# Four graph layers on one core: exponent rows through DMA, multi-head aggregation transposed for head pairs, new order of work

## What is computed

```python
h = relu(layernorm(x)); x = x + L0(h)     # one head: softmax(mask(leaky_relu(h W1 (h W2)^T))) (h W3), relu
h = relu(layernorm(x)); x = x + GAT(h)    # 4 heads of 64: e = leaky_relu(e_src_i + e_dst_j), softmax, elu
h = relu(layernorm(x)); x = x + MHA(h)    # 4 heads of 64, biases, output projection Wo, layernorm * gamma + beta
h = relu(layernorm(x)); x = x + GAT(h)    # as layer 1, other weights
```

## Time and profile before

| | before |
|---|---|
| median of 3 runs | 3149.03 us (3148.59 to 3149.07) |
| profiled execution | 3149.14 us, span of the core 3147.3 us |
| TensorE busy | 3024.6 us, 96% |
| VectorE busy | 2164.3 us, 69% |
| ScalarE busy | 1628.3 us, 52% |
| GpSimd busy | 765.3 us, 24% |
| mean granted TensorE clock | 0.988 |

### The profile page before, as it was taken

One profiled execution on the slowest core, in us unless ns is written; L12 is line 12 of the kernel. 1 busy time (PEld: TensorE's weight loads), 2 busy tenths in 40 slices (PEclk: granted clock), 3 DMA queues, 4 the chain that ended last, 5 costly groups with the idle time before them and its releaser, 6 DMA issues.

```text
span 3147.3 us, 83725 instructions
## 1 busy us (share of the span) xinstructions
PE 3024.6 (96%) x35494; PEld 2280.4 (72%) x35494; DVE 2164.3 (69%) x5660; ACT 1628.3 (52%) x3457; POOL 765.3 (24%) x917
## 2 busy tenths in 40 slices
PE   4799999999999999999999999999999999999985
PEld 2577777777777777777777777777777777777764
DVE  3467667667767767767766767766767776766764
ACT  1355555455455455455446555545555545555533
POOL 1222222222222222222222222222222222222221
...
GB/s 75 14 2 15 15 15 14 9 9 15 15 15 15 8 15 8 15 15 15 8 15 8 15 15 15 8 15 8 15 15 15 8 15 8 15 9 8 4 6 15
DMA packets 38420, 43.24 MB, mean 14 GB/s; under 512 B 2496, under 2 KB 37312, under 8 KB 38048
## 3 DMA queue, kind: packets, MB, share of 16 engines
...
## 4 chain that ended last, share of the span: by engine, by line
PE 92%; ACT 3%; DVE 2%; issue 1%; POOL 0%; DMA 0%; SPq 0%; POOLq 0%; DVEq 0%; ACTq 0%
PE ps L889 19%; PE ps L994 16%; PE ps L895 11%; PE ps L1045 8%; PE ps L1020 8%; PE ps L925 8%; PE ps L1029 7%; PE ps L946 7%; PE ps L979 4%; PE ps L880 3%; PE ps L934 2%; ACT hn L407 1%; ACT qT L533 1%; ACT qx L462 1%; DMA wqkvo<-in_L_gnn_Wo 0%
## 5 line engine op out<-in xcount | busy, mean ns | idle before, releaser
L724 DVE SCALAR_TENSOR_TENSOR pA<-ps,gval,adjT 128x512 f32<-128x512 f32 x512 | 357.8, 741 | 211.1 <-PE ps L979 211.1
L407 ACT ACTIVATE hn<-xc,nb,rstd 128x256 f32<-128x256 f32 x384 | 208.3, 591 | 327.3 <-DVE nb L640 327.3
L724 DVE SCALAR_TENSOR_TENSOR pB<-ps,gval,adjT 128x512 f32<-128x512 f32 x512 | 354.1, 738 | 1.0 <-PE ps L994 1.0
L330 POOL TENSOR_SCALAR rstd<-mv 128x4 f32<-128x4 f32 x160 | 36.6, 229 | 1177.0 <-DVE mv L632 1177.0
L994 PEld LDWEIGHTS ps<-vals,pA 128*64 128x64 f32 x8192 | 252.5, 139 | 81.8 <-issue 77.5
L994 PEld LDWEIGHTS ps<-vals,pB 128*64 128x64 f32 x8192 | 250.1, 138 | 80.7 <-issue 55.5
L994 PE MATMUL ps<-vals,pA 128*64 128x65 f32 x8192 | 270.2, 225 | 5.3 <-DVE pA L724 5.3
L343 POOL TENSOR_TENSOR vals<-qx,gval 128x256 f32<-128x256 f32 x256 | 153.7, 623 | 495.6 <-ACT gval L474 495.6
L889 PE MATMUL ps<-wgat,hT 128*128 128x264 f32 x1024 | 270.3, 399 | 3.7 <-ACT hT L416 3.5
L994 PE MATMUL ps<-vals,pB 128*64 128x65 f32 x8192 | 267.9, 224 | 4.3 <-DVE pB L724 2.6
L355 POOL TENSOR_TENSOR qx<-qx,xc 128x512 f32<-128x512 f32 x128 | 163.1, 1274 | 366.0 <-ACT qx L483 366.0
...
## 6 DMA issues: line engine op xcount, KB each, us to landing
x_in<-in_x SPq DMA_DIRECT2D x32, 512.0 KB, 4.0
out_x<-xc SPq DMA_DIRECT2D x32, 512.0 KB, 3.0
pX<-in_adj SPq DMA_DIRECT2D x1, 1024.0 KB, 5.7
...
```

The lines of the kernel that those rows point to most:

```text
L407: nc.scalar.activation(hn[s][:, t, :], src[:, t, :], ACT.Identity if norm == "in" else ACT.Relu, bias=nb[s][:, t:t + 1], scale=rstd[s][:, ...
L724: last = nc.vector.scalar_tensor_tensor(out=gat_p[s][h % 2][:, t, :], in0=ps[:, BANK[f"R{g}.{h}"], :], scalar=gval[s][:, 1, t, h:h + 1], i ...
```

## The change

The exponent rows of the GAT layers no longer come from 16 transposes per layer into PSUM. ScalarE writes the exponents to `grow` (128 x 16), one transpose and one VectorE copy make `growT` (16 x 128), SyncE stores it to DRAM (8 KB) and loads it back spread over all partitions into qT and hT of the item (2 x 512 KB); `gat_weights` reads these rows from SBUF. In layer 2, `aggregate2` computes the transposed result for a pair of heads, with the values stationary (64 columns, one head in each half of the output partitions) and 512 columns of weights moving. The reciprocals of the sums are copied side by side by ScalarE (`inverse_columns`), transposed by TensorE (`inverse_spread`), and copied out (`inverse_out`); `norm2` is then one multiplication per pair that writes qT directly, and `o_columns` and `o_transposed` go. The lists of all engines are ordered anew: the projection of layer 1 (with its transposes, copies and the maximum) is now issued in the pass of a instead of b, `plus_beta` is issued for b behind `deviation(a, 1)`, steps in the same matmul mode stand more often side by side, and all PSUM banks are assigned anew. `slot` has a fourth item d = n-3, for one wait. Below are the lines that are added; the lines that they take the place of stand in the kernel above.

```diff
+        gval = sets("gval", [P, 2, NT, H])
+        grow = sets("grow", [P, H, NT])
+        growT = sets("growT", [H * NT, P])
...
+        gat_r = [[qT[s][:, 0, :], qT[s][:, 1, :], hT[s][:, 0, :], hT[s][:, 1, :]] for s in range(SETS)]
+        r_dram = {g: [nc.dram_tensor(f"r_dram{g}_{s}", [H * NT, P], f32).ap() for s in range(SETS)] for g in (1, 3)}
...
+            def spread(w, g):
+                if w is None:
+                    return
+                s, rows_dram = w.s, r_dram[g][w.s]
+                rT_out[g].wait(sp, w)
+                sp.dma_start(rows_dram, growT[s][:, :]).then_inc(r_written[g].sem, 16)
+                r_written[g].wait(sp, w, 16)
+                for dst, first in ((qT[s], 0), (hT[s], 2)):
+                    src = rows_dram.rearrange("(o h t) p -> o h (t p)", o=1, h=H)[:, first:first + 2, :]
+                    sp.dma_start(dst[:, :, :], src.broadcast_to([P, 2, N])).then_inc(r_loaded[g].sem, 16)
+            def slot(a, b, c, more=True):
+                if more:
+                    load_next(a)
+                spread(a, 1); store(c); spread(b, 3)
...
+            def slot(a, b, c, d):
+                gat_values(b, 1); deviation(a, 0); deviation(c, "in"); residual2(c); deviation(c, 3)
+                gat_residual(b, 1, 0); gat_residual(b, 1, 1); deviation(b, 2); gat_values(c, 3)
+                residual0(a, 0); residual0(a, 1); deviation(a, 1); plus_beta(b); gat_residual(c, 3, 0)
...
+            def gat_row_exp(w, g):
+                if w is None:
+                    return
+                s = w.s
+                gexp_ready[g].wait(act, w, 3)
+                nc.scalar.activation(grow[s][:, :, :].rearrange("p h t -> p t h"), gexp[s][:, 1, :, :],
+                                     ACT.Exp).then_inc(grow_ready[g].sem, 1)
...
-                if h == 3:
+                if h == 3 and t == 1:
...
+            def inverse_columns(w, p):
+                if w is None:
+                    return
+                rinv2.wait(act, w, p + 1)
+                nc.scalar.copy(kT[w.s][:, p, :].rearrange("p (t h d) -> p t h d", t=NT, h=2),
+                               rinv[w.s][:, 2 * p:2 * p + 2, :].rearrange("p h t -> p t h").unsqueeze(3)
+                               .broadcast_to([P, NT, 2, D])).then_inc(invc_ready.sem, 1)
+            def inverse_out(w, p):
+                if w is None:
+                    return
+                invp_ready.wait(act, w, p + 1)
+                nc.scalar.copy(kT[w.s][:, p, :], ps[:, BANK[f"RB{p}"], :]).then_inc(inv_ready.sem, 1)
+            def slot(a, b, c, d):
+                exp2(c, 3, 3); inverse_columns(c, 0); gat_exp(b, 1); weights_out2(c, 2, 2)
+                inverse_columns(c, 1); weights_out2(c, 3, 1); weights_out2(c, 3, 3); inverse_out(c, 0)
...
+            def gat_rows_out(w, g):
+                if w is None:
+                    return
+                rT_ready[g].wait(dve, w)
+                nc.vector.tensor_copy(growT[w.s][:, :], ps[0:H * NT, BANK[f"RT{g}"], 0:P]).then_inc(rT_out[g].sem, 1)
...
-                    r_ready[g].wait(dve, w, h + 1)
-                    gval_ready[g].wait(dve, w, 1)
+                    if h == 0:
+                        r_loaded[g].wait(dve, w, 32)
...
-                        out=gat_p[s][h % 2][:, t, :], in0=ps[:, BANK[f"R{g}.{h}"], :],
+                        out=gat_p[s][h % 2][:, t, :], in0=gat_r[s][h],
...
+            def inverse_sums2(w, p):
+                if w is None:
+                    return
+                s = w.s
+                p2_ready[2 * p].wait(dve, w, NT)
+                p2_ready[2 * p + 1].wait(dve, w, NT)
+                hs = slice(2 * p, 2 * p + 2)
+                nc.vector.reciprocal(rinv[s][:, hs, :], rowsum[s][:, hs, :]).then_inc(rinv2.sem, 1)
+            def norm2(w, p):
+                if w is None:
+                    return
+                agg2_ready.wait(dve, w, p + 1)
+                inv_ready.wait(dve, w, p + 1)
+                nc.vector.tensor_tensor(qT[w.s][:, p, :], ps[:, BANK[f"G2.{p}"], :], kT[w.s][:, p, :],
+                                        ALU.mult).then_inc(oT_ready.sem, 1)
...
+            def slot(a, b, c, d):
+                weights_out2(c, 3, 0); weights_out2(c, 3, 2); statistics(a, 0); mean_and_variance(a, 0)
+                norm2(c, 0); shift_of_norm(a, 0); norm2(c, 1); gat_weights(b, 1, 0, 0, 1, 2, 3)
+                gat_weights(b, 1, 1, 0, 1); o_out(c); statistics(c, "in"); mean_and_variance(c, "in")
+                gat_weights(b, 1, 1, 2, 3); gat_weights(b, 1, 2, 0); shift_of_norm(c, "in")
+                gat_norm(b, 1, 0); gat_weights(b, 1, 2, 1, 2, 3); times_gamma(c); gat_weights(b, 1, 3, 0)
+                gat_norm(b, 1, 1); gat_weights(b, 1, 3, 1, 2); statistics(c, 3); mean_and_variance(c, 3)
+                gat_weights(b, 1, 3, 3); gat_norm(b, 1, 2); shift_of_norm(c, 3); masked_max0(a, 0)
+                masked_max0(a, 1); gat_norm(b, 1, 3); lrelu0(a, 0); gat_out(b, 1, 0); masked_max0(a, 2)
+                lrelu0(a, 1); gat_out(b, 1, 1); lrelu0(a, 2); masked_max0(a, 3); softmax_shift0(a)
+                statistics(b, 2); mean_and_variance(b, 2); lrelu0(a, 3); weights_out0(a, 1)
+                shift_of_norm(b, 2); gat_max_t(c, 3); gat_max(c, 3); gat_shift(c, 3); inverse_sum0(a)
+                weights_out0(a, 3); gat_rows_out(c, 3); statistics(a, 1); mean_and_variance(a, 1)
+                shift_of_norm(a, 1); gat_weights(c, 3, 0, 0, 1, 2); masked_max2(b, 0, 0, 0)
+                masked_max2(b, 0, 0, 1); masked_max2(b, 0, 1, 0); masked_max2(b, 0, 1, 1)
+                masked_max2(b, 1, 0, 0); masked_max2(b, 1, 0, 1); masked_max2(b, 0, 2, 0)
+                gat_weights(c, 3, 0, 3); masked_max2(b, 0, 2, 1); gat_weights(c, 3, 1, 0, 1, 2)
+                masked_max2(b, 0, 3, 0); gat_weights(c, 3, 1, 3); masked_max2(b, 0, 3, 1)
+                masked_max2(b, 1, 1, 0); gat_norm(c, 3, 0); softmax_shift2(b, 0); masked_max2(b, 1, 1, 1)
+                gat_weights(c, 3, 2, 0); gat_norm(c, 3, 1); gat_weights(c, 3, 2, 1); masked_max2(b, 1, 2, 0)
+                masked_max2(b, 1, 2, 1); masked_max2(b, 1, 3, 0); masked_max2(b, 1, 3, 1)
+                gat_weights(c, 3, 2, 2, 3); gat_weights(c, 3, 3, 0); softmax_shift2(b, 1)
+                gat_weights(c, 3, 3, 1); weights_out2(b, 1, 0); gat_weights(c, 3, 3, 2); gat_max_t(a, 1)
+                weights_out2(b, 0, 1); gat_max(a, 1); gat_norm(c, 3, 2); gat_weights(c, 3, 3, 3)
+                weights_out2(b, 1, 2); gat_shift(a, 1); weights_out2(b, 0, 3); gat_norm(c, 3, 3)
+                inverse_sums2(b, 0); weights_out2(b, 2, 1); gat_rows_out(a, 1); weights_out2(b, 2, 3)
+                gat_out(c, 3, 0); inverse_sums2(b, 1); gat_out(c, 3, 1)
...
+            def gat_rows(w, g):
+                if w is None:
+                    return
+                grow_ready[g].wait(pe, w)
+                nc.tensor.transpose(ps[0:H * NT, BANK[f"RT{g}"], 0:P], grow[w.s][:, :, :].rearrange("p h t -> p (h t)"),
...
+            def inverse_spread(w, p):
+                if w is None:
+                    return
+                invc_ready.wait(pe, w, p + 1)
+                for t in range(NT):
+                    cols = slice(t * P, (t + 1) * P)
+                    last = nc.tensor.transpose(ps[:, BANK[f"RB{p}"], cols], kT[w.s][:, p, cols], ident[:, :])
+                last.then_inc(invp_ready.sem, 1)
+            def aggregate2(w, p):
+                if w is None:
+                    return
+                s = w.s
+                if p == 0:
                     v2_ready.wait(pe, w)
+                for h in (2 * p, 2 * p + 1):
+                    pT2_act[h].wait(pe, w, 2)
+                    pT2_dve[h].wait(pe, w, 2)
+                for j in range(NT):
+                    for hh in range(2):
+                        h = 2 * p + hh
+                        last = nc.tensor.matmul(
+                            ps[hh * D:(hh + 1) * D, BANK[f"G2.{p}"], :],
+                            vals[s][:, j, h * D:(h + 1) * D],
+                            probT2[s][h][:, :, j * P:(j + 1) * P],
+                            start=(j == 0), stop=(j == NT - 1))
                 last.then_inc(agg2_ready.sem, 1)
...
+                    oT_ready.wait(pe, w, 2)
...
+            def slot(a, b, c, d):
+                gexp_ready[1].wait(pe, b, 2); weights_transposed2(c, 3, 0); weights_transposed2(c, 1, 3)
+                weights_transposed2(c, 2, 1)
+                pT2_act[1].wait(pe, c, 1); weights_transposed2(c, 3, 1); gat_rows(b, 1)
+                gnorm[3].wait(pe, d, 4); weights_transposed2(c, 2, 2)
+                pT2_dve[0].wait(pe, c, 2); weights_transposed2(c, 2, 3); aggregate2(c, 0)
+                weights_transposed2(c, 3, 2)
+                pT2_dve[2].wait(pe, c, 2); weights_transposed2(c, 3, 3)
+                pT2_act[2].wait(pe, c, 2); inverse_spread(c, 0); inverse_spread(c, 1); aggregate2(c, 1)
```

(47 more changed lines are left out.)

188 lines of the change are left out of this document (34 added, 154 removed), and 17 rows, old and new, of the table BANK.

## The result

The changed kernel takes 3165.8 us (median of 5 runs, 3163.1 to 3169.6), the kernel before 3148.7 (3148.6 to 3149.1): a ratio of 1.0055, 95% interval 1.0040 to 1.0069. That is 0.5% slower. The forecast was 3151, in a range of 3035 to 3220. The profiled execution has a span of 3164.0 us and a mean granted clock of 0.975, where it was 0.988.

What follows compares the result with a forecast made beforehand. TensorE was taken to bound the kernel: 88.2 us of work plus 5.4 of waits make a 93.6 us pass. 3147.3 - 7 for 30 passes + 9 at the edges + 1.8 gave 3151 us, range 3035 to 3220.

Steps and rivals of the forecast that it cites:

- What is late next: Full pass: waits of TensorE for VectorE's results, 5.4 us together, giving back the gain on TensorE.
- o_rows: Output step of item c: TensorE waits for norm2(c,1) behind one pair of transposes, 0.4 us per pass.
- head 3: First GAT layer: TensorE waits 1.95 us for head 3's weights, delayed by GpSimd's rstd (+1.4) and residual2 (+1.75).
- the next block: After head 3: TensorE waits 1.3 us for masked_max0(a,0), behind nb(c,3), which sits behind GpSimd's gat_residual.
- plus_beta: GpSimd's plus_beta (2.37 us), moved behind rstd(a,1), holds back nb(a,1); TensorE then waits 1.15 us for bank 0.
- TensorE's work: Matmul work per full pass: 88.2 us if nothing is late, 5.6 less than before.
- The clash: VectorE instructions with two SBUF inputs and GpSimd ones reading SBUF exclude each other; all 32 weights per pass are affected.
- milder clash: Rival, chance 0.37: rstd doesn't exclude VectorE, 3103 us; with weights not clashing at all, 3049.
- the half rate: Rival, chance 0.01: weights with two f32 SBUF sources run at half rate, 21 us more VectorE work per pass, 3943.
- The slower rival, the clock: Rival, chance 0.12: standing still after 32.2 us of each pass lowers TensorE's clock, 102 us in all, 3253.
- The edges: Filling and emptying, one or two items in flight: +9 us (end +5, filling +6, two-item pass -2), between 0 and 20.
- credits: At the end, 2 us off for rows VectorE needn't await and 2 for the shorter path from aggregate2 to the projection.

Runs made afterwards that it cites:

- e1: The changed kernel with plus_beta(b) moved ahead of residual0(a) in GpSimd's list, no longer behind deviation(a, 1): 3118.3 us.
- e4: The changed kernel with residual2 moved from GpSimd to VectorE, right behind times_gamma: 3128.4 us.
- e5: The changed kernel with plus_beta early, residual2 on VectorE, and gat_residual(b, 1, 0) ahead of deviation(c, 3) on GpSimd: 3052.0 us.
- e8: The changed kernel with plus_beta early and residual2 on VectorE, but gat_residual(b, 1, 0) still behind deviation(c, 3): 3083.3 us.
- e3: The kernel before with one of each row's four transposes kept and read four times by the weights, other rows left out of the result: 3076.5 us.
- e2: The kernel before with gat_weights reading its row operand from a constant SBUF tensor, not PSUM; rows still made but unused: 3263.9 us.
- e7: The changed kernel with plus_beta early and gat_residual(b, 1, 0) ahead of deviation(c, 3) on GpSimd, residual2 staying there: 3117.0 us.

## The prediction against the runs, point by point

- **What is late next: right in place and nearly in size.** Forecast and measured, in us: o_rows 0.4 and 0.24; head 3 1.95 and 1.95; the next block 1.3 and 1.08; plus_beta 1.15 and 1.25; smaller ones 0.6 and none over 0.2. Together 5.4 and 4.5. e1, e4 and the pair e5 and e8 show by removal that head 3, the next block and plus_beta are each a cost of its own (of head 3's, half was removed): 3165.8 goes to 3052.0, with the 8 us of the clock in it.
- **TensorE's work: mis-sized.** 93.55 - 4.52 = 89.0 of work where the steps gave 88.2. aggregate2 was better than taken: two heads run side by side (starts 10 ns apart below), 3.59 and 3.75 for the two blocks, 7.34 against 7.64. e3 prices the 30 transposes at 3.0, not 3.3. The rest, 0.8, must lie in the order and the small gaps, for which I had taken a gain of 0.4 and the end of all waits; no run separates these. The two errors, 0.8 too little work and 0.9 too much waiting, cancel, and so the 93.6 was as good as it looks partly by luck.

```profile
1503.21 0.59 PE L1103 MATMUL ps<-pX,vals 128*64 128x512 f32 x1
1503.22 0.59 PE L1103 MATMUL ps<-pA,vals 128*64 128x512 f32 x1
```

- **The clash: the right rule, drawn too wide.** Residual2, gat_residual and plus_beta exclude VectorE's instructions with two SBUF inputs. rstd doesn't: the rows above show a weight within it at its usual 0.74, and it is rstd that grows, by 0.30 and 0.35. I had put 1.4 us on it. Head 3 was as late as forecast all the same, and that was luck: residual2 cost 2.17 (2.91 - 0.74) and not 1.75, and 0.9 us of small pauses of VectorE (idle for 0.50, 0.27 and 0.15) had been left out. The rival "milder clash" had this half right; its price of 48 us came from taking the 1.4 off a sum that had other errors on the other side. It was summed wrong besides: 1.4 and 0.6 off 93.6 leave 91.6 and 3091 us, not 92.0 and 3103.
- **The weight from SBUF at 0.74: right.** The median is 743 ns in the changed kernel and 742 in e2, so the half rate that the Trainium skill states in "Vector Engine (DVE) Microarchitecture Reference", "Points that are easy to get wrong", isn't there, and the rival built on it falls.
- **The slower rival, the clock: right in mechanism and place, wrong in price.** It falls right behind the wait for head 3. But it falls in one pass of two and costs 0.4 to 0.7 us each time, since the next wait hides the rest: 8 us, not 102. In e7 it costs 27. I had let it decide the sign only if VectorE were a us later still, and given it 0.12; a small form of it belonged in the sum.
- **DMA: right.** The store took 1.3 us, at most 3.0 by the bound; the loads 4.0 and 4.9 against 5.7. They landed 3.6 us before the weights asked, not 1.4.
- **The edges: mis-sized, and this is the term that made the kernel slower.** +9 was taken and +18 measured, still within the bounds of 0 to 20. The filling, up to the projection of the first full pass, is 9.7 longer (197.8 for 188.1; forecast 6). The pass with two items takes 88.07 for 88.06 (forecast -2), and what follows its projection is 8.2 longer (64.0 for 55.8; forecast +5). In the filling VectorE's first weight comes at 112.7 instead of 104.6: 8.1 later, of which 1.5 were there before the rows began (the maximum is spread at 104.50, not 103.01), so that the detour shows in full, 6.6, and no part lies beside item 1. At the end the first weight comes 7.57 us behind gexp (3130.20 to 3137.77), where it came 1.16 behind (3121.16 to 3122.32): 6.4, against the 7.3 of the sum without its credits (3.0 + 5.7 + 0.6 less 2). So the price of the detour was nearly right; what failed were the credits set against it, the 2 for the shorter path from aggregate2, the 2 for the two-item pass and the cover in the filling.

  The detour's 6.6 and 6.4 are 13 of the 18 us. The clock has a part in the rest, for which the forecast had no term: the granted clock is 0.50 to 0.59 from 105 to 120 us, where it was 1.00 before, and the first aggregation takes 3.68 us for 2.09; behind the last detour two blocks take 3.30 and 3.33, where one took 3.74. No run has the changed kernel without its detour, so this split is read from the trace and not shown by removal.

DMA issues of the kernel after (columns as in the earlier trace rows):

```profile
qT<-r_dram SPq DMA_DIRECT2D x64, 512.0 KB, 4.0
hT<-r_dram SPq DMA_DIRECT2D x64, 512.0 KB, 4.9
...
r_dram<-growT SPq DMA_DIRECT2D x64, 8.0 KB, 1.3
```

In sum, the forecast of 3151 was 15 us too low: passes -1 where -7 was put (the clock's 8 us), edges +18 where +9 was put.
